# Key and value stage begun with column quarters of the weight, row tiles normed inside it, 17 graph groups in the query stage, a one-hot product on ScalarE

## The reference

```python
xn = layernorm(x)
W = zeros(1024, 1024).at[src, dst].add(edge_weight)
graph = xn @ W.T + gnn_bias
q, k, v = split(xn @ W_qkv); q = relu(rmsnorm(q, qn_w)); k = relu(rmsnorm(k, kn_w))   # 16 heads of 64
kv = einsum('hnd,hne->hde', k, v)
mix = (einsum('hnd,hde->hne', q, kv) / (einsum('hnd,hd->hn', q, k.sum(n)) + 1e-6)) @ W_out + b_out
x = x + graph + mix
t = rmsnorm(x) * norm_scale
x + sum over the 2 best of 8 experts of p_e * (swiglu(t @ w1_e + b1_e) @ w2_e + b2_e)
```

## Time and profile before

| | us |
|---|---|
| median of three runs | 1088.17 (1085.77 to 1089.17) |
| the profiled execution | 1088.06 |
| its span | 1086.3 |
| prologue, to TensorE's first key unit | 91.4 |
| key and value stage, to the first query unit | 292.3 |
| query stage, to the first matmul on the graph weight | 129.2 |
| the rest | 573.4 |

### The profile page before, as it was taken

One profiled execution on the slowest core, in us unless ns is written; L12 is line 12 of the kernel. 1 busy time (PEld: TensorE's weight loads), 2 busy tenths in 40 slices (PEclk: granted clock), 3 DMA queues, 4 the chain that ended last, 5 costly groups with the idle time before them and its releaser, 6 DMA issues.

```text
span 1086.3 us, 17104 instructions
## 1 busy us (share of the span) xinstructions
PE 944.4 (87%) x5425; PEld 588.4 (54%) x5426; DVE 733.2 (67%) x1190; ACT 297.6 (27%) x490; POOL 198.2 (18%) x226
## 2 busy tenths in 40 slices
PE   1537899999999999999999999997828999999992
PEld 1324566666666666555566666564524455455551
DVE  4887788888888887526887777675264555555551
ACT  0563222222222211524112222221102333333331
POOL 1124000000000000000333333222201333333321
PEclk9757899999999999999999999998859999999997
DMA  7455543333333440882115555655718987977543
GB/s 248 135 172 182 187 154 136 136 138 134 143 135 139 166 169 20 194 276 93 40 57 154 154 154 154 173 169 158 229 38 307 313 268 190 312 202 185 120 96 59
DMA packets 77818, 176.24 MB, mean 162 GB/s; under 512 B 24180, under 2 KB 39482, under 8 KB 73922
## 3 DMA queue, kind: packets, MB, share of 16 engines
q1 hardware_dynamic: 70001, 147.40, 41.1%
q0 software_dynamic: 7776, 28.32, 11.7%
HBM read 113.54 MB, written 62.67 MB: 162 GB/s over the span
## 4 chain that ended last, share of the span: by engine, by line
PE 34%; DVE 27%; DMA 14%; issue 10%; ACT 5%; POOL 3%; SPq 2%; DVEq 2%; ACTq 0%; POOLq 0%
PE bank L861 9%; PE windows L984 8%; DMA arena<-t_dram,arena 6%; DMA arena<-in_w_flat 6%; PE bank L1002 3%; DVE arena L1358 2%; DVE arena L1370 2%; DVE arena L1476 2%; DMA out_x<-arena 2%; DVE arena L1378 2%; PE bank L884 2%; DVE arena L1353 2%; DVE arena L1356 2%; PE bank L890 2%; PE bank L975 2%
## 5 line engine op out<-in xcount | busy, mean ns | idle before, releaser
L766 PE MATMUL bank<-arena 128*125 128x512 f16 x960 | 216.3, 382 | 0.0
L766 PEld LDWEIGHTS bank<-arena 128*125 (+1 forms) x960 | 129.0, 138 | 72.5 <-issue 2.7
L984 PE MATMUL windows<-arena 128*128 x648 | 148.5, 379 | 0.2 <-issue 0.2
L884 PE MATMUL bank<-arena 128*125 128x512 f16 x432 | 98.0, 384 | 9.2 <-DVE arena L1512 7.6
L861 PE MATMUL bank<-arena 128*128 128x416 f16 (+1 forms) x576 | 104.2, 339 | 0.0
L984 PEld LDWEIGHTS windows<-arena 128*128 128x128 f16 x648 | 63.4, 98 | 65.1 <-issue 0.4
L890 PE MATMUL bank<-arena 128*125 128x512 f16 x432 | 95.8, 379 | 0.0
L884 PEld LDWEIGHTS bank<-arena 128*125 128x125 f16 x432 | 59.5, 138 | 44.1 <-DVE arena L1512 8.1
L861 PEld LDWEIGHTS bank<-arena 128*128 128x128 f16 x576 | 55.5, 97 | 44.5 <-issue 0.4
L1538 DVE SCALAR_TENSOR_TENSOR arena<-arena 128x512 f16<-128x512 f32 x40 | 40.8, 1021 | 57.5 <-ACT arena L1178 57.4
L890 PEld LDWEIGHTS bank<-arena 128*125 128x125 f16 x432 | 59.0, 137 | 33.4
(11 more groups left out here) (244 smaller groups left out, 1479.0 us busy)
## 6 DMA issues: line engine op xcount, KB each, us to landing
arena<-split_dram SPq DMA_DIRECT2D x56, 512.0 KB, 7.1
arena<-in_w_flat SPq DMA_DIRECT2D x22, 1024.0 KB, 6.4
split_dram<-arena SPq DMA_DIRECT2D x44, 512.0 KB, 3.6
arena<-in_w_flat SPq DMA_DIRECT2D x40, 256.0 KB, 3.9
split_dram<-arena SPq DMA_DIRECT2D x80, 128.0 KB, 2.2
arena<-in_x SPq DMA_DIRECT2D x20, 448.0 KB
arena<-in_w_qkv SPq DMA_DIRECT2D x8, 1024.0 KB, 6.2
t_dram<-arena SPq DMA_DIRECT2D x10, 448.0 KB
```

The source lines that it names most:

```text
L766: mm = pe.matmul(bank[b][0:TT, :], xt[:, l, k, tok(i)], wkv[:, r, k, c0:c0 + 512], start=(k == 0 and n == 0), stop=(k == KT - 1 and n == 2))
L884: pe.matmul(o[half][0:TT, :], xt[:, l, k, tok(i)], wg[:, r, k, c0:c0 + 512], start=(k == 0 and c == 0), stop=False)
L984: mm = pe.matmul(bank[6][:, :], rowT[s][:, l, k, :], arena16[:, bass.ds(off + (r * KT + k) * 512, 512)], start=(k == 0 and c == 0), stop=( ...
```

## The change

- The key and value weight is loaded in eight parts of a quarter of the columns by half of the rows (1 MB each, in three `wide` buffers). A unit of tile 0 waits only for the two parts of its quarter. VectorE splits the lows of parts 0, 1, 2, 4 and 6, GpSimd of 3, 5 and 7.
- Only tile 0 is normed and transposed before the stage. The transposed halves of tile i+1 and the statistics and norm of tile i+2 stand inside tile i.
- The edge table is made between the work for tiles 0 and 1, its matmuls stand inside tile 1, and tiles 0 and 1 have no graph groups. Tiles 2 to 9 have four each, and the 17 others stand in the query stage, one behind each of the units 0 to 10 and one in the middle of units 1, 3, 5, 7, 9 and 10. The splits of `w_acc` begin at unit 11.
- The product of the key's one-hot matrix with the high weight leaves VectorE: ScalarE does it in eight operations of 128 columns, one for each step of the group (`hot_scale`).
- The 22 early pieces are handled as 44 halves, four in tile 1 and five in each of the tiles 2 to 9. SyncE loads the first query weight behind the last store.
- ScalarE zeroes `w_acc`, at the end of tile 1. The loops over tiles are written out.

```diff
-KV_GROUPS = 4 * NT
+KV_GROUPS = 4 * (NT - 2)
...
-        key16 = S([STEPS], F16); lo16 = S([STEPS], F16); whi = S([STEPS], F16); wlo = S([STEPS], F16)
+        key16 = S([STEPS], F16); lo16 = S([STEPS], F16); whi = S([STEPS]); wlo = S([STEPS], F16)
         slot_at = S([STEPS], I32); base_at = S([GROUPS + 2], I32)
+        one_hot_at = S.at
         one_hot = [S([3, G * P], F16) for _ in range(2)]
         stage_at = S.at
-        stage = [S([PIECE]) for _ in range(2)]
+        stage = [S([HALF]) for _ in range(2)]
+        xs_late = [S([D]) for _ in range(2)]
         wq_first = S([2, KT, P], F16)
...
-        part = [B([2, PIECE], F16) for _ in range(2)]
-        wide = stage + [p.rearrange("p a b -> p (a b)").bitcast(F32) for p in part]
...
+        part = [B([2, HALF], F16) for _ in range(2)]
+        wide = [view(one_hot_at, [PIECE]), view(stage_at, [PIECE]), view(B_AT, [PIECE])]
...
+        LO_ON_POOL = (3, 5, 7)
...
+        HALVES_OF = [0, 4] + [5] * (NT - 2)
+        assert sum(HALVES_OF) == 2 * EARLY
...
+        Q_AT = {}
+        for u in range(11):
+            if u in (1, 3, 5, 7, 9, 10):
+                Q_AT[u, "mid"] = KV_GROUPS + len(Q_AT)
+            Q_AT[u, "end"] = KV_GROUPS + len(Q_AT)
+        assert len(Q_AT) == Q_GROUPS
+        FIRST_SPLIT = 11
+        def splits(unit):
+            return range(max(3 * (unit - FIRST_SPLIT), 0), min(3 * (unit - FIRST_SPLIT) + 3, KT))
...
+            def load_wkv(m):
+                q, below = divmod(m, 2)
+                if m >= 3:
+                    wait_wkv_lo(sp, m - 3)
+                sp.dma_start(wide_part(m), kv_rows[:, 4 * below:4 * below + 4, D + q * 512:D + (q + 1) * 512]).then_inc(wide_in[m % 3], 16)
+            load_x(0)
+            load_wkv(0)
+            load_wkv(1)
             sp.wait_ge(edges_in, 1)
...
+            load_x(1)
+            sp.dma_start(knw, kn_w.partition_broadcast(P)).then_inc(knw_in, 16)
+            load_wkv(2)
+            load_wkv(3)
+            load_x(2)
+            load_wkv(4)
+            load_x(3)
+            for m in (5, 6, 7):
+                load_wkv(m)
...
+            ask(0)
+            ask(1)
+            for i in range(NT):
+                for n in halves(i):
+                    store(n)
+                    if n + 2 < 2 * EARLY:
+                        ask(n + 2)
+                if i + 5 < NT:
+                    load_x(i + 5)
...
-                sp.wait_ge(part_out[h], 32 * N_PIECE_Q // 2)
+                sp.wait_ge(part_out[h], 32 * N_PIECE_Q)
             load_wq(0, 0)
-            store(EARLY - 2, 0)
             sp.wait_ge(kv_mm, 4 * NT)
             load_wq(0, 1)
-            store(EARLY - 1, 1)
             for h in range(2):
-                sp.wait_ge(part_out[h], 32 * EARLY // 2)
+                sp.wait_ge(part_out[h], 32 * EARLY)
+            sp.wait_ge(kv_used, START + NT)
...
-            pool.wait_ge(table_done, 1)
-            for k in range(KT):
-                pool.memset(w_acc[:, k * D:(k + 1) * D], 0.0).then_inc(acc_zero, 1)
+            for m in LO_ON_POOL:
+                pool.wait_ge(wkv_hi, m + 1)
+                pool.tensor_tensor(wkv_part(1, m), wide_part(m), wkv_part(0, m), ALU.subtract).then_inc(wkv_lo_p, 1)
...
+            pe.wait_ge(xn_ready, 1)
+            xt_half(0, 0)
+            xt_half(0, 1)
+            pe.wait_ge(xt_done, 2)
+            wait_wkv_lo(pe, 1)
+            kv_unit(0, 0, 0)
+            first_counts()
+            wait_wkv_lo(pe, 2)
+            wait_wkv_lo(pe, 3)
+            kv_unit(0, 1, 512)
+            wait_wkv_lo(pe, 4)
+            wait_wkv_lo(pe, 5)
+            kv_unit(0, 2, 1024)
+            pe.wait_ge(xn_ready, 2)
+            pe.wait_ge(kw_ready, 1)
+            xt_half(1, 0)
+            xt_half(1, 1)
+            wait_wkv_lo(pe, 6)
+            wait_wkv_lo(pe, 7)
+            pe.wait_ge(kw_ready, 2)
+            kv_unit(0, 1, 1536)
+            any_kv = wkv[:, 0, 0, 0:512]
+            pe.wait_ge(xt_done, 4)
+            kv_unit(1, 0, 0)
+            for b in range(3):
+                pe.matmul(bank[3 + b][:, :], zeros, any_kv, start=True, stop=False, skip_group_check=True)
...
+            pe.wait_ge(table_done, 1)
+            for i in range(2, NT):
+                n = 4 * (i - 2)
+                pe.wait_ge(xt_done, 2 * i + 2)
                 kv_unit(i, 0, 0)
-                slot = step_slots(4 * i)
-                if not first:
-                    pe.wait_ge(v_lo, 2 * i)
-                    kv_sums()
-                steps(4 * i, 0, slot)
+                slot = step_slots(n)
+                pe.wait_ge(v_lo, 2 * i)
+                kv_sums()
+                steps(n, any_kv, slot)
                 kv_unit(i, 1, 512)
-                steps(4 * i + 1, 1)
+                steps(n + 1, any_kv)
+                if i + 1 < NT:
+                    pe.wait_ge(xn_ready, i + 2)
+                    pe.wait_ge(kw_ready, 2 * i + 1)
+                    xt_half(i + 1, 0)
                 kv_unit(i, 2, 1024)
-                steps(4 * i + 2, 0)
+                steps(n + 2, any_kv)
+                if i + 1 < NT:
+                    pe.wait_ge(xt_done, 2 * i + 3)
+                    xt_half(i + 1, 1)
                 pe.wait_ge(kw_ready, 2 * i + 2)
                 kv_unit(i, 1, 1536)
-                steps(4 * i + 3, 1)
-            kv_tile(0, True)
-            with pe.Fori(1, NT) as i:
-                kv_tile(i)
+                steps(n + 3, any_kv)
             pe.wait_ge(v_lo, 2 * NT)
             kv_sums()
...
+            def piece_hi(n):
+                if n < 2:
+                    wait_wkv_lo(a_, 7)
+                    wait_wkv_lo(a_, 6)
+                a_.wait_ge(stage_in[n % 2], 16 * (n // 2 + 1))
+                if n >= 2:
+                    a_.wait_ge(part_out[n % 2], 32 * (n // 2))
+                a_.activation(part[n % 2][:, 0, :], stage[n % 2], ACT.Copy, scale=SW).then_inc(part_hi, 1)
+            def hot_scale(n):
+                pairs_of = one_hot[n % 2][:, 1, :].rearrange("p (a k j) -> p a k j", a=G // 2, j=2)
+                a_.wait_ge(hot_key, 2 * n + 2)
+                for j in range(G):
+                    col = pairs_of[:, j // 2, :, j % 2]
+                    ins = a_.activation(col, col, ACT.Copy, scale=whi[:, n * G + j:n * G + j + 1])
+                ins.then_inc(hot_ready, 1)
...
-            def kv_tile(i, t, h):
-                k_half(i, 0)
-                piece_hi(1 + 2 * t + h, 0)
-                k_half(i, 1)
...
+            piece_hi(0)
+            v_half(1, 0)
+            hot_scale(0)
+            ln_sqrt(3)
+            xt_hi_half(2, 1)
+            piece_hi(1)
+            v_half(1, 1)
+            a_.wait_ge(table_done, 1)
+            for k in range(KT):
+                a_.activation(w_acc[:, k * D:(k + 1) * D].rearrange("p (a b) -> p a b", b=P), zeros.unsqueeze(1).to_broadcast([P, KT, P]), ACT.Copy).then_inc(acc_zero, 1)
+            hot_scale(1)
+            piece_hi(2)
+            piece_hi(3)
+            for i in range(2, NT):
+                n, hs = 4 * (i - 2), halves(i)
+                k_half(i, 0)
+                hot_scale(n + 2)
+                piece_hi(hs[0])
+                k_half(i, 1)
+                k_root(i)
+                hot_scale(n + 3)
+                if i + 1 < NT:
+                    xt_hi_half(i + 1, 0)
+                piece_hi(hs[1])
                 a_.wait_ge(k_rs, i + 1)
                 v_half(i, 0)
-                piece_hi(1 + 2 * t + h, 1)
+                hot_scale(n + 4)
+                piece_hi(hs[2])
+                if i + 2 < NT:
+                    ln_sqrt(i + 2)
+                if i + 1 < NT:
+                    xt_hi_half(i + 1, 1)
+                piece_hi(hs[3])
                 v_half(i, 1)
-            with a_.Fori(0, NT // 2) as t:
-                for h in range(2):
-                    kv_tile(2 * t + h, t, h)
+                hot_scale(n + 5)
+                piece_hi(hs[4])
...
+                    if (6 * t + u, "mid") in Q_AT and Q_AT[6 * t + u, "mid"] + 2 < GROUPS:
+                        hot_scale(Q_AT[6 * t + u, "mid"] + 2)
...
-                cols = lambda a: a[:, bass.ds(n * G, G)].rearrange("p (a j) -> p a j", j=2).unsqueeze(2).to_broadcast([P, G // 2, P, 2])
-                v.tensor_tensor(pairs_of(one_hot[s][:, 0, :]), columns, cols(lo16), ALU.is_equal)
-                v.wait_ge(hot_ready, n)
+                cols = lambda a: a[:, n * G:(n + 1) * G].rearrange("p (a j) -> p a j", j=2).unsqueeze(2).to_broadcast([P, G // 2, P, 2])
                 key_hot = pairs_of(one_hot[s][:, 1, :])
                 v.tensor_tensor(key_hot, columns, cols(key16), ALU.is_equal).then_inc(hot_key, 1)
+                v.tensor_tensor(pairs_of(one_hot[s][:, 0, :]), columns, cols(lo16), ALU.is_equal)
                 v.wait_ge(hot_key, 2 * n + 1)
                 v.tensor_tensor(pairs_of(one_hot[s][:, 2, :]), key_hot, cols(wlo), ALU.mult).then_inc(hot_key, 1)
-                v.wait_ge(hot_key, 2 * n + 2)
```

(58 more changed lines are left out.)

443 lines of the change are left out of this document (223 added, 220 removed).

## The result

| | kernel before | changed kernel |
|---|---|---|
| median, us (runs) | 1088.67 (4) | 1167.31 (4; 1166.16 to 1170.8) |
| ratio to before | | 1.0732, 95% interval 1.0714 to 1.0750 |
| span of the profiled execution, us | 1086.3 | 1165.7 |
| first unit of the query stage, us | 383.71 | 448.04 |
| four window additions of a steady tile, us | 28.54 | 41.45 |

The change makes the kernel 7.3% slower. The windows of the changed kernel show where: stretch, length, busy of TensorE, its weight loads, VectorE, ScalarE and GpSimd, then granted clock, DMA share, GB/s.

The account below looks back on a forecast made before the run. VectorE was taken to set the key and value stage's period, TensorE 1 us behind. 1088.06 + 55.8 to the query stage + 1.5 cold unit + 10.8 group steps + 2.7 late weight = 1159 us; range 1120 to 1190.

Parts of the forecast that it names:

- VectorE's own work in the new tile: Key and value stage: VectorE's operations alone take 29.9 us a tile, against 28.55 before.
- Eight products: ScalarE's eight 128-column products with the high weight, 0.29 us apart, take 2.4 us for a group.
- rival of cheap products: Small ScalarE operations follow each other at 0.18 us, so each wait is 0.9 shorter: 1130 us; 8 in 100.
- The waits: VectorE waits for ScalarE at four places a tile, together 12.2 us, making the period 42.1 us.
- the rival that they are hidden: VectorE's waits are hidden, so the stage runs at 29.9 or 28.6 us a tile: 1062 us; 7 in 100.
- The start: Before the steady tiles: first window addition at 103.5 us, 8 either way.
- The bound of 50: Start: the weight's parts are all split at 37 us at the earliest, up to 50; 49 was taken.
- To the query stage: From the first window addition, seven periods, the last tile and a load: first query unit at 439.5 us, +55.8.
- The first query weight: End of the key and value stage: loaded only behind the last store, two issues of 0.9 and 0.8, landing 3.4 us.
- The query stage: Eight more group steps of 1.35 us on TensorE, +10.8; late weight loads, +2.7; cold first unit, +1.5.
- The late weight: Query stage: later weight loads add 2.7 us, bounds 0 and 6, the larger of two delays.
- TensorE's clock: Rival: waits throttle TensorE; 36.7 us a tile if partly slow, 1279 us in total if slow throughout; 3 in 100.

Follow-up runs that it names:

- e2: Changed kernel with each group's eight ScalarE products one place later in its queue, behind the high halves: 1068.12 us, 0.9809 of before.
- e3: Changed kernel with ScalarE doing only four of a group's eight products (graph weight wrong, prices the product only): 1125.95 us, one run.
- e6: e5 with the third to fifth weight parts asked for ahead of row tiles 1 to 3 and the key norm's weight: 1047.35 us.
- e5: e4 with the zeroing of the window sums moved from ScalarE back to GpSimd: 1056.41 us, 0.9701 of before.
- e4: e2 with SyncE loading the first query weight ahead of the last tile's stores instead of behind them: 1059.07 us, 0.9721 of before.
- e8: e5 with GpSimd's three low parts given to VectorE, which also takes three scalings off ScalarE: 1059.21 us, ratio 0.9733.

## Why the prediction was right, and where its steps were off

The time was 1167.31, forecast 1159 with a range of 1120 to 1190, and the mechanism is the one forecast: 95 of the 99 us between the changed kernel and e2 are eight periods of 41.45 instead of 29.52. That the sum came as near as 8 us is in part luck: it was 8.5 too small up to the query stage and 4.1 in it, and 4.0 too large behind it. And by the prediction's own sign (the first addition within 8 of 103) its start was wrong. Step by step:

- **VectorE's own work in the new tile**, forecast 29.9: 41.45 less 12.1 of waits is 29.4. e2, where the waits are gone, has 29.52, with 0.44 of a wait that hangs on TensorE.
- **Eight products**, forecast 2.4: 2.48, and 0.29 apart by e3, as worked out. The rival of cheap products falls.
- **The waits**, forecast 3.5, 3.0 + 0.3, 1.9, 3.5: measured 3.46, 2.99 + 0.26, 1.91, 3.46. The period was forecast at 42.1 and is 41.45. e2 shows that they are a matter of order alone; the rival that they are hidden falls for the kernel as changed, and e2 is what that rival would have looked like.
- **The start** is the step that was too small: the first window addition came at 116.43, forecast 103.5 with 8 either way. 9.7 of the 12.9 us arise before all parts are split: I took 49 and the last two units begin at 58.68.

```profile
35.13 7.90 PE L790 MATMUL bank<-arena 128*125 128x512 f16 x24 [8.18 <-POOL arena L656]
...
58.68 13.25 PE L790 MATMUL bank<-arena 128*125 128x512 f16 x48 [6.81 <-POOL arena L656]
```

  The step took the landing from the earlier trace rows, 6.2 us a part. In the changed kernel it is 9.5, with the third part and what follows issued among row tiles and the edge table's loads. The order of issue alone gave 10.3 us at the first window addition (e6), of which the loads themselves are an estimated 3 to 5. Of about the same size is a second term, which the step had at nothing: a pick of VectorE takes 4.42 in place of 0.64 beside GpSimd's subtraction, and ScalarE's split waits behind it. The profile before shows such a price, a norm that took 2.86 where the one in the earlier trace rows took 0.81, while the subtraction of the earlier trace rows ran (57.27 to 61.33):

```profile
59.03 2.86 DVE L1315 TENSOR_SCALAR arena<-arena 125x1024 f32<-125x1024 f32 x1
```

  The bound of 50 had been worked out from the split's own chain and left out both. The last two units and the table after them took 39.8 (the window above) where 37.6 was said, with a granted clock of 0.93. The zeroing, costed at 7.9, was about 3 on the path (e5), because a load stood behind it.
- **To the query stage**: from the first window addition to that of the last tile 289.5 (405.96 - 116.43) for 293.7 forecast, from there to the last piece low 36.9 for 37.2, and 5.2 from there to the first query unit for 5.1. So 12.9 late at the start, 4.4 won back, 8.5 at the query stage: 448.04 against 439.5.
- **The first query weight** behind the last store: e4 shows 9.0 us for it, of which 6.8 is the wait and 1.5 the slower unit. The prediction had it as a part of its walk, not as a term; with the order of the parts (e6) it was the second largest thing to be won.
- **The query stage**, forecast +15.0, measured +19.1. The first unit is 6.98 long where the same one took 4.24 in the earlier trace rows, so 2.7 for a cold start in place of 1.5 (and the pair that the prediction gives for its 1.5, 6.1 against 5.3, differs by 0.8 only):

```profile
448.04 6.98 PE L943 MATMUL bank<-arena 128*128 128x418 f16 x24 [10.00 <-DMA arena<-split_dram]
...
541.91 18.78 PE L943 MATMUL bank<-arena 128*128 128x418 f16 x96 [2.17 <-DMA arena<-split_dram]
```

  The late weight stands as its second row, 2.17 for 2.7. It is the query weight, for which the walk had 1.9 (462.2 less 460.3); the 2.7 were for the output weight, and no fold waited for a load. With 10.8 for the steps that is 15.7. Of the other 3.4 some 0.8 are TensorE's waits for products (L815), and a unit cut by a group step takes 2.27 twice where an uncut one takes 4.38, 0.16 for each cut. What is left, about 1 to 2 us, I can't assign.
- **What lies behind**, forecast unchanged, was 4.0 shorter. No run was made on it and its cause is open.
- **TensorE's clock** was no bound. The tile's granted clock is 0.88, TensorE is busy 31.70 for a forecast of 36.7, and ran at the higher of its two levels for most of it. After the tile's longest wait a zeroing pair took 1.01 where it takes 0.59 after a short one:

```profile
242.35 0.59 PE L815 MATMUL windows<-arena 128*128 128x512 f16 x2 [1.01 <-DVE arena L1493]
253.80 1.01 PE L815 MATMUL windows<-arena 128*128 128x512 f16 x2 [4.33 <-DVE arena L1493]
```

  This drop is inside a chain that VectorE sets, and VectorE waits for TensorE nowhere in this tile, so it cost nothing. In e2, without the waits, the granted clock is 1.00.

**A version that beats both.** e6 holds the change's gain (an early stage, a shorter `make`) without its loss: 1047.35 us, 3.8% faster than before (0.9622, 0.9588 to 0.9656). It consists of three moves in orders and one to another engine: products one place later (-99 us), the first query weight ahead of the last stores (-9), weight parts ahead of row tiles (-9), and the zeroing on GpSimd (-3 by the medians, which is within the noise).

## What to carry to other kernels

When work is handed to an idle engine, ask what stands behind it in that engine's queue: the price was not the 2.48 us of work on an engine that was idle for half of the tile, but that the work waits for its input while the thing its supplier needs next stands behind it. Here the two queues asked each other in turn, and so ran one after the other; the same operations one place later, behind what the other side needs, cost VectorE no wait. And a landing time read in one order of issue didn't hold in another (6.2 us before, 9.5 in the changed kernel, 7.3 in e6): walk the DMA queue for what is issued around the load, as one walks an engine's. Last, when an experiment gives more than its theory allows, as e6 did, compare every engine's time line before crediting the theory.

## What the runs showed of the hardware that I had not expected

- A GpSimd subtraction of 128x2048 (4.06 us) held up a VectorE operation on 128x408 fp32 from 0.64 to 4.41 us, and one on 125x512 from 0.69 to 2.69; with GpSimd's subtractions gone (e8) neither is long. One that reads a bank (L1504, 125x512) ran beside the same subtraction in its usual 0.69, so not every operation is held. In e6, where the same subtraction stands elsewhere, other operations are the long ones: a low half of 128x2048 took 3.98 where it takes 2.29. What the held ones have in common was not tested. GpSimd's eight memsets of 128x1024 fp32 (7.20 us, at 90.08 in e5) ran beside VectorE with no operation of VectorE over 1.3 us.
- Eight 1 MB loads of the same shape landed in a median of 9.5 us in the changed kernel, 9.7 in e5 and 7.3 in e6, by the order in which they and the loads around them were issued.
- After a wait of 6.82 us the first query unit took 6.17, after one of 10.00 us 6.98, with no wait directly ahead 4.71: a long gap in TensorE's work costs a second time behind it. A short one need not: after 0.78 us in e2 a key unit took 5.39, where it takes 5.34 with none.
